# Weights by values on two column tiles of 64, high and low weights side by side

## The reference

```python
q = _split_heads(jnp.einsum('bnd,df->bnf', x, Wq))
kv = jnp.einsum('bmc,cf->bmf', context, Wkv)
k, v = jnp.split(kv, 2, axis=-1)
k, v = (_split_heads(k), _split_heads(v))
...
sim = jnp.einsum('bhid,bhjd->bhij', q, k)
attn = jax.nn.softmax(sim, axis=-1)
out = jnp.einsum('bhij,bhjd->bhid', attn, v)
```

## Time and profile before

| what | value |
|---|---|
| median of 3 executions | 3195.95 us |
| lowest, highest | 3195.18, 3199.17 us |
| the profiled execution | 3188.72 us |
| its span, first to last instruction | 3187.0 us |
| mean granted clock of TensorE | 0.965 |
| stage `ca` | about 1380 to 2670 us of the span |

### The profile page before, as it was taken

One profiled execution on the slowest core, in us unless ns is written; L12 is line 12 of the kernel. 1 busy time (PEld: TensorE's weight loads), 2 busy tenths in 40 slices (PEclk: granted clock), 3 DMA queues, 4 the chain that ended last, 5 costly groups with the idle time before them and its releaser, 6 DMA issues. The chain is left out here.

```text
span 3187.0 us, 40194 instructions
## 1 busy us (share of the span) xinstructions
PE 2927.5 (92%) x17029; PEld 1615.4 (51%) x17029; DVE 1505.5 (47%) x1769; ACT 1011.6 (32%) x1525; POOL 68.9 (2%) x189
## 2 busy tenths in 40 slices
PE   6999999988989999989999999999999997627799
PEld 3334444433444444456666666666666664415453
DVE  5359999994643222323434343434343421376410
ACT  3354434423423222322323232323232321283210
POOL 1000000000000000000000000000000000010000
PEclk9999999999999999999999999999999998868899
DMA  5133343333323333535555454546464542111203
GB/s 202 49 107 93 93 138 91 102 122 119 122 87 115 103 104 100 160 88 112 139 113 144 113 144 111 144 111 140 113 147 112 117 85 75 54 30 37 105 4 142
DMA packets 472619, 341.52 MB, mean 107 GB/s; under 512 B 232212, under 2 KB 437333, under 8 KB 467832
## 3 DMA queue, kind: packets, MB, share of 16 engines
q1 hardware_dynamic: 472440, 338.95, 39.1%
HBM read 226.60 MB, written 54.62 MB: 88 GB/s over the span
## 5 line engine op out<-in xcount | busy, mean ns | idle before, releaser
L366 PE MATMUL vw_pv<-vw_wv,vw_ctx 128*128 128x512 f16 (+1 forms) x1232 | 471.5, 383 | 34.3 <-PEq L73 15.1
L367 PE MATMUL vw_pv<-vw_wv,vw_ctx 128*128 128x512 f16 (+1 forms) x1232 | 470.9, 382 | 0.0
L368 PE MATMUL vw_pv<-vw_wv,vw_ctx 128*128 128x512 f16 (+1 forms) x1232 | 470.9, 382 | 0.0
L1449 PE MATMUL ca_p_s<-early_halves,ca_qw 128*128 128x448 f16 (+2 forms) x1408 | 466.8, 332 | 1.4 <-DVE ca_qw L1562 1.4
L1451 PE MATMUL ca_p_s<-early_halves,ca_qw 128*128 128x448 f16 (+2 forms) x1408 | 466.8, 332 | 0.0
L1450 PE MATMUL ca_p_s<-early_halves,ca_qw 128*128 128x448 f16 (+2 forms) x1408 | 466.8, 332 | 0.0
L1562 DVE TENSOR_TENSOR ca_qw<-ca_p_w,ca_qw 128x512 f16<-128x512 f32 x128 | 88.5, 691 | 546.0 <-ACT ca_qw L1512 546.0
L386 DVE TENSOR_TENSOR vw_vst<-vw_pv,vw_vst 128x512 f16<-128x512 f32 (+1 forms) x154 | 105.5, 687 | 334.4 <-ACT vw_vst L377 334.3
L1512 ACT ACTIVATE ca_qw<-ca_p_w 128x512 f16<-128x512 f32 x128 | 76.4, 597 | 559.2 <-PE ca_p_w L1430 559.2
L377 ACT ACTIVATE vw_vst<-vw_pv 128x512 f16<-128x512 f32 (+1 forms) x154 | 90.9, 593 | 408.7 <-PE vw_pv L368 408.6
L366 PEld LDWEIGHTS vw_pv<-vw_wv,vw_ctx 128*128 128x128 f16 (+1 forms) x1232 | 121.2, 98 | 190.9 <-issue 28.0
(11 more groups left out here) (447 smaller groups left out, 4803.8 us busy)
## 6 DMA issues: line engine op xcount, KB each, us to landing
vw_ring<-in_ctx_t SPq DMA_DIRECT2D x109, 512.0 KB, 3.8
vd<-vw_vst SPq DMA_DIRECT2D x192, 256.0 KB, 2.3
ca_vals<-vd SPq DMA_DIRECT2D x64, 768.0 KB
ca_stage<-in_ctx_t SPq DMA_DIRECT2D x91, 512.0 KB, 3.5
ex_w_d<-in_w_d SPq DMA_DIRECT2D x8, 2048.0 KB, 7.2
early_r<-state_rows SPq DMA_DIRECT2D x8, 1024.0 KB, 7.8
early_r<-in_w SPq DMA_DIRECT2D x2, 4096.0 KB, 13.1
vw_ring<-in_w_kv SPq DMA_DIRECT2D x8, 512.0 KB, 4.3
```

The lines of the kernel that those rows point to most:

```text
L366: self.nc.tensor.matmul(o, xh[:, c, 0:w], self.wv[0][:, c, f], start=(c == 0), stop=False)
L367: self.nc.tensor.matmul(o, xh[:, c, 0:w], self.wv[1][:, c, f], start=False, stop=False)
L368: last = self.nc.tensor.matmul(o, xl[:, c, 0:w], self.wv[0][:, c, f], start=False, stop=(c == CC - 1))
L1449: nc.tensor.matmul(o, a[:, 0, c, :], x[:, 0, c, lo:hi], start=(c == 0), stop=False)
```

## The change

The stationary operand is no longer 128 columns of values but 64, those of one head, and the product of head 0 goes to output partitions 0 to 63, that of head 1 to 64 to 127. In the compiled program these matmuls have an array tile of 128 rows by 64 columns, at column 0 or 64. The moving operand of the first matmul is the 64 high and the 64 low weights of that head, side by side as 128 columns (a view with two runs of 64), so that high by high and high by low come out of one matmul in neighbouring columns; the low values by high weights are a second matmul of 64 columns onto the first 64. Per tile of keys there are four matmuls with four loads where there were three with three. The two column halves of `p_o` are added at the end: `leave` is now a scaling copy of 128 partitions, a wait on a new semaphore `o_first`, and a multiply and add of the other half onto it. `av_done` counts two per pair instead of one, and those who wait for it count accordingly.

```diff
@@ load_values, turn
-                    sp.wait_ge(av_done, f - 1)
+                    sp.wait_ge(av_done, 2 * (f - 1))
@@ attend_to
-                o, v, a = p_o[:, p * P:(p + 1) * P], vals[f % 2], turned[f % 2]
+                v, a = vals[f % 2], turned[f % 2]
+                heads = [slice(h * DH, (h + 1) * DH) for h in range(2)]
+                o = [p_o[h, 2 * p * S:2 * (p + 1) * S] for h in heads]
                 for j in range(JT):
                     w = tile_rows(j) + (j == JT - 1)
-                    nc.tensor.matmul(o, v[0:w, j, 0, :], a[0:w, 0, j, :], start=(j == 0), stop=False)
-                    nc.tensor.matmul(o, v[0:w, j, 0, :], a[0:w, 1, j, :], start=False, stop=False)
-                    last = nc.tensor.matmul(o, v[0:w, j, 1, :], a[0:w, 0, j, :], start=False, stop=(j == JT - 1))
-                last.then_inc(av_done, 1)
+                    for i, h in enumerate(heads):
+                        nc.tensor.matmul(o[i].rearrange("p (l s) -> p l s", l=2), v[0:w, j, 0, h], a[0:w, :, j, h],
+                                         start=(j == 0), stop=False)
+                    for i, h in enumerate(heads):
+                        last = nc.tensor.matmul(o[i][:, 0:S], v[0:w, j, 1, h], a[0:w, 0, j, h], start=False,
+                                                stop=(j == JT - 1))
+                        if j == JT - 1:
+                            last.then_inc(av_done, 1)
@@ leave
-                dve.wait_ge(av_done, (G + 1) * GP)
+                dve.wait_ge(av_done, 2 * (G + 1) * GP)
                 dve.wait_ge(q_ready, 2 * (G + 1) * GP)
-                for h in range(2):
-                    ins = nc.vector.tensor_scalar(
-                        o_t[h * DH:(h + 1) * DH, b, g * GP:(g + 1) * GP, :],
-                        p_o[h * DH:(h + 1) * DH, :].rearrange("p (c h s) -> p c h s", h=2, s=S)[:, :, h, :],
-                        1.0 / (W_UP * P_UP), None, ALU.mult)
-                ins.then_inc(o_copied, 1)
+                both = p_o[:, :].rearrange("p (c l s) -> p l c s", l=2, s=S)
+                o = o_t[:, b, g * GP:(g + 1) * GP, :]
+                nc.vector.tensor_scalar(o, both[:, 0, :, :], 1.0 / (W_UP * P_UP), None, ALU.mult).then_inc(o_first, 1)
+                dve.wait_ge(o_first, G + 1)
+                nc.vector.scalar_tensor_tensor(o, both[:, 1, :, :], 1.0 / (W_UP * P_UP), o, ALU.mult,
+                                               ALU.add).then_inc(o_copied, 1)
```

More of the change, by code:

```diff
@@ L1318, in attend @@
         half_done, peak_done, max_done, exp_done, sum_done, inv_done, wh_done, wl_done, av_done, o_copied, ctx_high, \
-            ctx_low, q_zero, q_ready, qw_ready, qw_high, qw_low, pad_zero, ld_null, null_high, null_low, null_set = \
+            ctx_low, q_zero, q_ready, qw_ready, qw_high, qw_low, pad_zero, ld_null, null_high, null_low, null_set, o_first = \
             st.sems("half_done peak_done max_done exp_done sum_done inv_done wh_done wl_done av_done o_copied ctx_high "
-                    "ctx_low q_zero q_ready qw_ready qw_high qw_low pad_zero ld_null null_high null_low null_set")
+                    "ctx_low q_zero q_ready qw_ready qw_high qw_low pad_zero ld_null null_high null_low null_set o_first")
         ld = [st.sem(f"ld{s}") for s in range(3)]
```

## The result

The changed kernel took 3146.93 us (median of 4, 3143.41 to 3150.01) where the kernel before took 3195.56 (median of 4, 3189.53 to 3199.17): a ratio of 0.9849, 95% interval 0.9831 to 0.9868, or 1.5% less time. Timed again on another occasion it was 3152.95 us against 3192.59, ratio 0.9871 (0.9848 to 0.9893). The prediction was 3160.8 us with a range of 3150 to 3240; the measured median lies 3.1 us under its lower end and beside rival 1 (3146.6 us). The direction was right, the size was not.

A forecast was written before the change was run, and what follows sets the result against it. TensorE's own steps were taken to bound `attend`: 56 visits, each 0.63 us shorter (2.18 to 1.55), give -35.3 us and `leave` +0.1, so 3195.95 - 35.2 = 3160.8 us, range 3150 to 3240.

The forecast's parts named there:

- rival 1: In `attend_to`, loads keep up (fast or hidden): 85.1 ns per tile of keys, visit 1.30 us, kernel 3146.6 us; chance 0.13.
- What bounds the stage: In `attend`, TensorE's own steps set the time: busy 159.59 of 160 us, with all other work of the pair hidden.
- The stream of matmuls: Per tile of keys in `attend_to`: 167.7 ns before; after, 170.2 if matmuls run alone, 85.1 if side by side.
- The loads: In `attend_to`, 64-column loads at 52.3 ns, two in sequence per column tile, set the step: 104.6 ns per tile of keys.
- Column tiling and the fast load: For `attend_to`'s loads, the skill's rule that column tiling excludes fast weight load; without it the forecast would be the fast rival.
- The change of mode: Each visit to `attend_to` enters 64-column tiles and goes back: 0.19 us per visit, between 0.1 and 0.3.
- Which visits count: Of 64 visits in `attend`, 56 gain: not the seven at later batch starts, nor pair 62's, behind which TensorE idles 9.24 us.
- The last visit: Pair 63's visit, after 9.24 us of TensorE idle, counted among the 56 at the ordinary gain of 0.63 us.
- `leave` and semaphores: `leave` at the stage's end: two instructions of 0.43 us and a 0.1 wait, +0.1 us (-0.2 to +0.4); semaphores 0.
- Sum: For the whole kernel: -35.3 us from visits and +0.1 from `leave`, -35.2 us, giving 3160.8 us.
- Rivals 2, 3 and 4: Tiles not side by side, 3208.5 us (0.10); narrow loads exposed, 3222.7 (0.11); all loads on one slow path, 3238 (0.19).

## Why the prediction missed, point by point

- *What bounds the stage.* Right: TensorE's steps; 0.82 us off each visit came off each gap of an undisturbed pair.
- *The stream of matmuls.* Right: 85.1 ns side by side, 87 measured; 170.2 one behind the other, 174 to 175 measured in the run on one tile. What makes up the 2 to 5 ns more isn't shown.
- *The loads.* This is the step that failed. The term was 52.3 ns per load and tile; it measured 31 to 32. With that, two loads of a tile take 63 ns and hide under 85. The size had two supports, and neither held. The first was the 209 ns step of the earlier trace rows, halved for two passes and taken as 0.82 ns per column. That row ran at the lower clock. The view by stretch (columns as in the earlier trace rows) gives a granted clock of 1.00 for it, but its 128-column f32 loads last 333 ns, and the loads of L594 right behind it change from one level to the other while nothing else changes:

```profile
24.30:29.10 4.80, 4.80 (x25) 4.80 (x24) 2.27 (x5) 4.65 (x9) 3.51 (x10) 1.00 0.00 0
```

```profile
L586 PEld LDWEIGHTS dp_p_work<-dp_lens,ones x24: 333/333/333, 24.1 to 29.0; 128*128 128x128 f32 x24
```

```profile
32.00 0.34 PEld L594 LDWEIGHTS dp_p_out<-early_halves,work 128*128 128x128 f32 x1 [0.52 <-issue]
32.85 0.34 PEld L594 LDWEIGHTS dp_p_out<-early_halves,work 128*128 128x128 f32 x1 [0.52 <-issue]
33.58 0.19 PEld L594 LDWEIGHTS dp_p_out<-early_halves,work 128*128 128x128 f32 x1 [0.39 <-issue]
34.01 0.19 PEld L594 LDWEIGHTS dp_p_out<-early_halves,work 128*128 128x128 f32 x1 [0.24 <-issue]
```

Up to 32.85 us such a load lasts 0.34 us and its matmul of 512 columns steps in 0.85; from 33.58 us on they take 0.19 and 0.43, and 0.43 is the step of the earlier trace rows. `attend` runs at the higher level, so the price for it is about half: an estimate from these rows is 209 / 2 / 2 = 52 ns per pass of 128 columns, 26 for 64. With 26 the same sum gives rival 1. The second support was the 8-column f16 load, which I had put on the f32 loads' line (81 + 0.8 per column) because 87 ns lies on it. But at 8 columns a line of 0.8 and one of 0.4 ns per column differ by 3 ns: that row couldn't choose between them, and the 0.8 are those of a whole f32 load, whose matmul goes through twice. The sign that I had named, 133 ns for the forecast and under 100 for rival 1, was off for both: the loads last 110 to 113 ns and hide. That the loads of the two tiles run independently, the other half of the choice, was right (63 against 127 ns).
- *Column tiling and the fast load.* The Trainium skill's page TensorEngine Tiling (Array Packing), under Restrictions and Gotchas, excludes the fast weight load in column tiles. The trace agrees: 64 columns hold the tile for 31.7 ns, when 128 columns of the full tile, with a matmul, pass in 27. No run here loads 64 f16 columns outside a column tile, so whether the tile or the width makes the load slower per column stays open. It changed nothing, since the load is hidden either way.
- *The change of mode.* Right in size: 0.09 us in, 0.02 in the first tile of keys and 0.10 out, 0.22 in all beside 0.19; the extra change cost 0.23 with its matmul, where 0.22 was expected.
- *Which visits count.* Right in kind: seven batch starts and pair 62 gained nothing, and the run without splits gives the full 51 us. The swallowed part should be 7 x 0.82 = 5.7 us; it came out at 8.6 in one trace and 5.1 in the other.
- *The last visit.* Missed: it gained some 1.8 us instead of 0.63 (from 2664.90 to the copy's start 4.09 us, now from 2622.99 to 2625.32, 2.33 us). It begins after 9 to 10 us of idle time, on the lower clock: before the change the granted clock from 2664 to 2672 us was 0.71, and most of that visit's matmuls stepped in 0.107 us, nearly twice the others' 0.056; after it the clock from 2622 to 2630 us was 0.50 and a tile of keys took 0.16 us, nearly twice 87 ns. At half the clock the same columns save twice the time.
- *`leave` and semaphores.* Right: two instructions of 0.42 us each, 0.46 from start to start, end 0.88 us after the start instead of 0.86.
- *Sum.* With 0.82 instead of 0.63 the same sum gives 56 x 0.82 = 45.9 us; 44.0 were measured in the stage, and 47.5 in the second trace. The median moved by 48.6 and, in the second timing, by 39.6; single executions scatter by up to 12 us. So that the first median lies within 0.4 us of rival 1 is in part luck: that rival has a visit of 1.30 us where 1.35 was measured, and a gain of 49.4.
- *The range* stopped between forecast and rival 1, which had a chance of 0.13: it cut off a rival of nearly the right time although the only objection to it was the price of the load above, 52.3 ns where 31.7 was measured.
- *Rivals 2, 3 and 4* fell: no load was exposed, and none went one behind another's tile.

## What to carry to other kernels

A matmul whose output is wanted only in 64-column blocks can run as two column tiles at once and halve its stream, even with twice as many, narrower loads, as long as the loads of each tile (31.7 ns for 64 f16 columns here) stay under that tile's matmuls; going into the narrow mode and back costs 0.2 us, so a visit should be long against that. Before a price is taken from a row, see on which clock it ran: compare the duration of an instruction that also stands elsewhere in the trace (here 333 and 190 ns for one kind of load), and don't rest on the granted clock alone. When a price is taken from a row at the far end of its scale, work out what the rival line would give at the same row: if the two differ by less than the row's scatter, it is no evidence, and the range must take both. Count the places where another chain sets the time: here 8 of 64 visits gave back their gain.

## What the runs showed of the hardware beyond that

A shorter pair can cost clock. At the start of the last batch TensorE now waits 2.35 us, and the granted clock in the stretch behind it fell to 0.67 (columns: start:end, length, engines, clock, DMA share, GB/s):

```profile
2451.00:2466.00 15.00, 15.00 (x104) 8.87 (x101) 7.96 (x7) 6.61 (x7) 1.56 (x2) 1.00 0.73 215
2467.40:2469.70 2.30, 0.00 (x0) 0.00 (x0) 1.08 (x3) 1.15 (x3) 0.00 (x0) 1.00 0.00 0
2469.80:2475.00 5.20, 5.20 (x27) 2.91 (x27) 2.11 (x4) 2.80 (x4) 0.00 (x0) 0.67 0.00 0
2475.00:2480.00 5.00, 5.00 (x42) 3.42 (x41) 2.81 (x4) 0.60 (x1) 0.30 (x2) 1.00 1.04 195
```

The 24 score matmuls behind the null key, which take 3.6 us elsewhere, took 5.3 there (2469.80 to 2475.07), so part of them ran at the lower of the two levels, 1.2 GHz, and that pair lost 1.7 us (gap 20.74 instead of 19.06). Of the seven waits, 1.02 to 2.35 us long, only the longest had this behind it; the one of 2.20 us had not, and before the change, with waits of at most 1.0 us, none had. The length of the wait alone doesn't decide it: the same 1.7 us stood behind a wait of 0.80 us in the run with 8 columns on one tile and behind 1.43 and 1.48 in that on two tiles, and not behind 1.84 in the run with the other order of the tiles. And two tiles of the array take their matmuls independently of how the program alternates them: head 1's first matmul started beside head 0's first though another of head 0 stood between them (6 ns apart by their starts in the trace of that run).
